# A graph network on one core: chunks, turned weights, copies and a residual put in another order and on other engines

## The chip, the cores and the metric

The kernel runs on one core of a Trainium2 chip. A core has TensorE (PE, products into PSUM), VectorE (DVE), ScalarE (ACT), GpSimd (POOL), and SyncE (SP), which here issues the transfers. Each engine takes its own instructions in the order in which they are written and waits on semaphores for the others. The metric is the device time of one execution in microseconds (us), lower is better.

## What is computed

The input x has 64 items of 128 rows and 512 nodes. Two graph layers follow each other, each with a residual and a layer norm over the nodes; the first one's graph is built from x itself (names as in the kernel):

```python
# layer 0; adj (128 x 128) is its weight, bias per row
x_norm = xn / max(norm(xn, axis=-1), 1e-12)              # xn: nodes, items, rows
S = einsum('nbl,mbl->nm', x_norm, x_norm) / B            # 512 x 512 likeness of nodes
A = S where it is among the k = 153 largest of its row (self left out), else 0
deg = A.sum(axis=0); An = rsqrt(deg)[:, None] * A * rsqrt(deg)[None, :]
out = einsum('sd,sbl->dbl', An, einsum('nbl,lo->nbo', xn, adj)) + bias
h = layernorm(x + out)
# layer 1, on h: two graphs of the 128 rows of each item
z_l = h @ W_lang.T; z_g = h @ W_grav.T; v = h @ W_V.T
K = w * rownorm(relu(cos(z_l, z_l))) + (1 - w) * rownorm(exp(-dist2(z_g) / (2 sigma^2)))  # causal
out = layernorm(h + (K @ v) @ W_O.T)
```

## The kernel before

Float32 operands are split in two float16 parts, high and low, and a product is three matmuls (`three`, lines 265 to 267): high by high, high by low, low by high. ScalarE mostly writes the high part, VectorE or GpSimd the low one (raw less high). The program has three stages; within a stage every engine's order is written out by hand.

1. **First pass** (to about 101 us). x comes in 16 chunks of 4 items (each chunk 4 slices of 128 x 512, `xn_h`, `xn_l`). PE's `rows_01` adds rows 0 and 1 of the block matrix S (banks 0, 1) chunk by chunk, as chunks are normalised.
2. **The stage of this change** (to about 204 us). PE finishes the diagonal blocks of rows 0 and 1 (`finish_diagonal`, lines 553 and 554: it adds the cross products high by low and their transpose, which ScalarE has copied out, `cross_out`, line 1007). ScalarE writes S (`s_out`, line 1002). PE turns five blocks (`turn`, line 559) and ScalarE copies them (line 1031). Then comes the **second pass**: `gram` for rows 2 and 3 of all 16 chunks, from what lies in SBUF (lines 523, 538, 544, 545, in the banks named pair23). Beside it VectorE searches the 153 largest entries of rows 0 and 1 (`pick(0)`: mean and deviation, whose root ScalarE takes, `deviation`, line 1026; three counts, line 1452; the eight next ones out, lines 1498 to 1507; a number loaded in a register, line 1526 is the first instruction behind it; then a loop) and makes A (`keep`, line 1550). Magnitudes of the inputs go over PE twice (lines 618 and 622) and give the scales (line 1568), after which ScalarE splits W_V and W_O (lines 1046, 1048), the adjacency, and group 0's x (lines 1058, 1063), with low parts by GpSimd (line 414). With the second pass done, rows 2 and 3 are finished in the same way and searched (`fill` lines 1585 to 1592, `pick(1)`, `keep(1)`). Beside that search PE turns W_grav (`turn_weight`, line 667; `less_high`, line 673, leaves the low part in the bank), makes W_V x W_O (`vo_product`, out by `vo_out`, lines 1133 and 1135), x times adjacency (`first_project`, out by lines 1074 and 1077), the upper blocks of W_grav's own product (`upper_product`), and sums the degrees (line 870). `needs_along` (line 610) turns the numbers that the search needs for its register. Behind the degrees (DVE line 1599) A is scaled and split, W_lang is turned, `mix_nodes` multiplies x's products with A, and group 0's y is made: bias and scale by ScalarE (`add_bias`, line 1098), x added by GpSimd (`residual`, line 438), statistics (line 1692), two factors, norm (line 1188), PE turns h (line 723), ScalarE and VectorE split it (lines 1278, 1880).
3. **16 groups of 4 items** (`body`) for the second layer and the next group's first layer. Here the first step that needs another engine's late work is group 1's x: high part by ScalarE (line 1083), low part by VectorE (line 1392), then `project_group`.

SP's transfers that lie in the stage: the first x (line 308) once W_V's low part is made, and the same x again into `xg[0]` (line 310) once the second pass is done.

## Time and profile before

| | us |
|---|---|
| median of 3 runs | 951.38 |
| lowest, highest | 951.23, 953.14 |
| profiled execution | 956.53 |
| its span | 954.8 |
| PE busy | 921.0 |
| VectorE busy | 752.5 |
| ScalarE busy | 535.4 |
| GpSimd busy | 312.8 |
| mean granted clock of PE | 0.989 |

The span goes from the first to the last instruction of the profiled execution. The matmul's own end is modelled in these records, and consecutive ones overlap: where PE is not waiting, the distance between starts is what a step costs. The granted clock is a share of 2.4 GHz; 0.5 is 1.2 GHz. The name in brackets behind a row of the timeline is the instruction whose end released the row's first one, with the idle time of the engine before it.

### The profile page before, as it was taken

The page shows a single profiled execution, that of the slowest core. Times are in us where ns is not written, and L with a number is a line of the kernel's source. Part 1 is how long each engine was busy: PE and PEld are TensorE (multiplying, and loading weights), DVE is VectorE, ACT ScalarE, POOL GpSimd, SP SyncE. Part 2 cuts the span into 40 slices and gives each one's busy share as a digit, 9 for nine tenths or more (in the row PEclk, how much of TensorE's full clock was granted, in tenths as well). Part 3 has the DMA queues.
Part 4 walks back from the last instruction along what each step waited for, and adds up shares of the span by engine and source line. Part 5 has one row for each costly group of instructions (what it writes and reads, how often), then busy time and mean ns, then how long its engine had stood idle before and what let it go on. Part 6 is the DMA issues. An engine that isn't in the chain of part 4 may idle for free.

```text
span 954.8 us, 19036 instructions
## 1 busy us (share of the span) xinstructions
PE 921.0 (96%) x6858; PEld 542.5 (57%) x6858; DVE 752.5 (79%) x1716; ACT 535.4 (56%) x976; POOL 312.8 (33%) x435
## 2 busy tenths in 40 slices
PE   8999899899999999999999999999999999999993
PEld 7777787455555555556464646455555455555451
DVE  5887488768888888878787888888887878786766
ACT  6887556685555555555546464646373636463531
POOL 5888162244040404040505050505050504040410
PEclk9999899999999999999999999999999999999997
DMA  7554120001323232314141413232222323231211
GB/s 301 187 204 150 43 90 25 34 32 21 80 67 78 67 83 60 95 48 109 34 120 28 115 33 109 40 103 46 96 53 90 57 86 60 85 56 45 56 45 44
DMA packets 101848, 75.84 MB, mean 79 GB/s; under 512 B 80560, under 2 KB 80688, under 8 KB 99888
## 3 DMA queue, kind: packets, MB, share of 16 engines
q1 hardware_dynamic: 101808, 75.32, 27.4%
q8 instruction: 24, 0.39, 0.2%
q14 instruction: 16, 0.13, 0.0%
HBM read 38.86 MB, written 16.78 MB: 58 GB/s over the span
## 4 chain that ended last, share of the span: by engine, by line
issue 51%; PE 21%; POOL 14%; DVE 8%; ACT 5%; DMA 1%; POOLq 1%; DVEq 0%; ACTq 0%
POOL arena L438 6%; PE bank L265 2%; PE bank L267 2%; PE bank L266 2%; PE bank L538 2%; POOL arena L443 2%; POOL arena L477 2%; PE bank L545 1%; PE bank L544 1%; ACT arena L1188 1%; POOL rn_parts L460 1%; DVE stats L1692 1%; POOL part_rest L458 1%; PE bank L508 1%; PE pair L265 1%
## 5 line engine op out<-in xcount | busy, mean ns | idle before, releaser
L265 PE MATMUL bank<-arena 128*128 128x512 f16 (+2 forms) x1056 | 293.8, 302 | 7.3 <-DVE arena L1746 2.7
L267 PE MATMUL bank<-arena 128*128 128x512 f16 (+2 forms) x1056 | 293.5, 302 | 0.0
L266 PE MATMUL bank<-arena 128*128 128x512 f16 (+2 forms) x1056 | 293.5, 302 | 0.0
L265 PE MATMUL pair<-arena 128*128 128x512 f16 (+1 forms) x400 | 151.1, 378 | 0.0
L266 PE MATMUL pair<-arena 128*128 128x512 f16 (+1 forms) x400 | 150.8, 377 | 0.0
L267 PE MATMUL pair<-arena 128*128 128x512 f16 (+1 forms) x400 | 150.7, 377 | 0.0
L265 PEld LDWEIGHTS bank<-arena 128*128 128x128 f16 x1056 | 103.5, 98 | 69.4 <-DVE arena L1746 5.0
L267 PEld LDWEIGHTS bank<-arena 128*128 128x128 f16 x1056 | 103.7, 98 | 63.3 <-issue 0.3
L266 PEld LDWEIGHTS bank<-arena 128*128 128x128 f16 x1056 | 103.7, 98 | 54.7 <-issue 0.3
L460 POOL TENSOR_TENSOR sq_parts<-cf,zero 128x4 bf16<-128x4 f32 x16 | 3.3, 208 | 399.4 <-DVE cf L1795 399.4
L438 POOL TENSOR_TENSOR arena<-arena 128x512 f32<-128x512 f32 x64 | 81.0, 1267 | 60.2 <-ACT arena L1098 59.8
L1199 ACT ACTIVATE arena<-bank 128x512 f16<-128x512 f32 x64 | 37.6, 589 | 96.7 <-PE bank L267 96.7
L443 POOL TENSOR_TENSOR arena<-arena 128x512 f16<-128x512 f32 x60 | 69.3, 1156 | 55.6 <-ACT arena L1193 53.6
L406 POOL TENSOR_TENSOR arena<-arena 128x512 f16<-128x512 f32 x64 | 72.8, 1160 | 21.4 <-ACT arena L976 21.4
L267 PEld LDWEIGHTS pair<-arena 128*128 128x128 f16 x400 | 39.1, 98 | 46.5 <-issue 0.3
L1746 DVE SCALAR_TENSOR_TENSOR arena<-bank,arena 128x512 f16<-128x512 f32 x64 | 43.9, 688 | 27.1 <-ACT arena L1199 27.1
L265 PEld LDWEIGHTS pair<-arena 128*128 128x128 f16 x400 | 39.1, 98 | 45.5 <-issue 0.5
L266 PEld LDWEIGHTS pair<-arena 128*128 128x128 f16 x400 | 39.2, 98 | 42.8 <-issue 0.5
L1188 ACT ACTIVATE arena<-arena,ln 128x512 f32<-128x512 f32 x64 | 51.3, 804 | 18.1 <-DVE ln L1718 18.1
L1392 DVE SCALAR_TENSOR_TENSOR arena<-arena,up 128x512 f16<-128x512 f32 x60 | 43.8, 774 | 19.3 <-ACT arena L1083 19.3
L1204 ACT ACTIVATE arena<-bank 128x512 f16<-128x512 f32 x32 | 19.1, 596 | 69.3 <-PE bank L267 69.3
L1692 DVE BATCH_NORM_STATS2 stats<-arena 128x6 f32<-128x512 f32 x64 | 44.1, 690 | 9.1 <-POOL arena L438 8.9
(344 smaller groups left out, 1943.0 us busy)
## 6 DMA issues: line engine op xcount, KB each, us to landing
arena<-in_x SPq DMA_DIRECT2D x32, 1024.0 KB, 5.5
out_dram<-arena SPq DMA_DIRECT2D x15, 1024.0 KB, 4.3
arena<-arena SPq DMA_TRANSPOSE x75, 3.2
arena<-in_x SPq DMA_DIRECT2D x2, 512.0 KB, 4.6
arena<-in_w_grav_t SPq DMA_DIRECT2D x1, 1024.0 KB, 7.3
arena<-in_w_lang_t SPq DMA_DIRECT2D x1, 1024.0 KB, 5.2
arena<-in_w_v SPq DMA_DIRECT2D x1, 1024.0 KB, 8.2
arena<-in_w_o_t SPq DMA_DIRECT2D x1, 1024.0 KB, 9.1
```

Source lines behind the costliest of these rows:

```text
L265: pe.matmul(dst, ah, bh, start=start, stop=False)
L266: pe.matmul(dst, ah, bl, start=False, stop=False)
L267: return pe.matmul(dst, al, bh, start=False, stop=stop)
L406: pool.tensor_tensor(xn_l[:, c * CL + t, :], xc[c % SLOTS][:, t, :], xn_h[:, c * CL + t, :], ALU.subtract).then_inc(s["xn_l_ready"], 1)
L438: pool.tensor_tensor(y[:, b, :], y[:, b, :], xg[slot][:, b, :], ALU.add).then_inc(s["y_ready"], 1)
L443: pool.tensor_tensor(h_l[:, b, :], h[slot][:, b, :], h_h[:, b, :], ALU.subtract).then_inc(s["hl_ready"], 1)
L1188: act.activation(h[slot][:, b, :], y[:, b, :], ACT.Identity, scale=ln1[:, 3, b:b + 1], bias=ln1[:, 4, b:b + 1]).then_inc(s["h_ready"], 1)
L1199: act.activation(z_h[i][:, E_ORDER[n], :, :], bank[n][:].rearrange("p (b n) -> p b n", b=GB), ACT.Copy, scale=U_DOWN).then_inc(done, 1)
L1204: act.activation(half_h[i], bank[4 + i][:].rearrange("p (b n) -> p b n", b=GB), ACT.Copy, scale=HALF_DOWN).then_inc(done, 1)
L1392: low = dve.scalar_tensor_tensor(x_l[:, b, :], xg[slot][:, b, :], up[:, 5:6], x_h[:, b, :], ALU.mult, ALU.subtract)
L1692: dve.bn_stats(stats[:, b, :], y[:, b, :]).then_inc(s["stat1_steps"], 1)
L1746: dve.scalar_tensor_tensor(z_l[i][:, e, :, :], bank[n][:].rearrange("p (b n) -> p b n", b=GB), U_DOWN, z_h[i][:, e, :, :], ALU.mult, ALU.s ...
```

## The change

- PE: rows 2 and 3 of chunk 0 are computed before the diagonals of rows 0 and 1, those of chunk 1 between diagonals and turns. The magnitude steps follow chunks 4 and 6 (were 2 and 4), the needs' transpose chunk 12 (was 9). W_grav's first turned weight stands before the diagonals of rows 2 and 3, the second before their turn. W_V's products 0 to 2 come ahead of x's products, which all stand behind the transpose of the second search's needs and use banks 0 to 3.
- ScalarE: four of the six fills of the second search's work area; x's scaling and high part behind S and a turned weight's high part; W_V's products out ahead of x's; the second search's root behind both; the bias added to group 0's x in place, in two steps of two items; in the last part, the turned h's first two high parts ahead of the norms of items 2 and 3, and W_lang's first copy behind them.
- VectorE: in a search, the register's steps are put between the two replacements, and the load beside the second; two of six fills stay; group 0's y is one step each from the bank (product times scale plus biased x), and the columns of constants are moved between these steps.
- GpSimd: no residual for group 0.
- SP: nothing in its code.

On PE, from the end of the first pass (rows 0, 1: bank0, bank1) into the second pass (pair23). L553 and L554 are the diagonals, L559 the turns. Before:

```order
L553 MATMUL bank0<-rinv_rep,ident 128x128
L554 MATMUL bank0<-ident,rinv_rep 128x128
L553 MATMUL bank1<-rinv_rep,ident 128x128
L554 MATMUL bank1<-ident,rinv_rep 128x128
L559 MATMUL bank7<-ident,arena 128x128
L559 MATMUL bank5<-ident,arena 128x128 x2
L559 MATMUL bank6<-ident,arena 128x128 x2
L538 MATMUL pair23<-arena 128x256
L523 MATMUL pair23<-arena 128x128
L544 MATMUL pair23<-arena 128x128
```

After, where L550 and L551 are the diagonals and L556 the turns; the rows left out repeat the slices of a chunk:

```order
L535 MATMUL pair23<-arena 128x256
L520 MATMUL pair23<-arena 128x128
L541 MATMUL pair23<-arena 128x128
...
L550 MATMUL bank0<-rinv_rep,ident 128x128
L551 MATMUL bank0<-ident,rinv_rep 128x128
L550 MATMUL bank1<-rinv_rep,ident 128x128
L551 MATMUL bank1<-ident,rinv_rep 128x128
L520 MATMUL pair23<-arena 128x128
L535 MATMUL pair23<-arena 128x256
...
L556 MATMUL bank7<-ident,arena 128x128
L556 MATMUL bank5<-ident,arena 128x128 x2
L556 MATMUL bank6<-ident,arena 128x128 x2
```

Two chunks of the second pass moved ahead, one before the diagonals and one before the turns.

On ScalarE, from x's scaling to the root of the second search (L1026, the last row). Before:

```order
L1058 ACTIVATE arena<-arena,up 128x2048
L1007 ACTIVATE rinv_rep<-pair23 128x128 x2
L1063 ACTIVATE arena<-arena 128x2048
L1002 ACTIVATE arena<-pair23 128x256
L1002 ACTIVATE arena<-pair23 128x128
L1070 ACTIVATE arena<-bank7 128x128
L1111 ACTIVATE arena<-bank4 128x512
L1111 ACTIVATE arena<-bank5 128x512
L1026 ACTIVATE guess<-guess 128x2
```

After, from the cross copies to the same root, now L1023; L1139 and L1142 are x, L1103 the low parts of two turned weights, L1121 and L1123 W_V's first product:

```order
L999 ACTIVATE arena<-pair23 128x128
L1027 ACTIVATE arena<-pair23 128x128
L1027 ACTIVATE arena<-bank7 128x128
L1136 ACTIVATE arena<-bank7 128x128
L1099 ACTIVATE arena<-bank5 128x512
L1139 ACTIVATE arena<-arena,up 128x2048
L1142 ACTIVATE arena<-arena 128x2048
L1103 ACTIVATE arena<-bank4 128x512
L1103 ACTIVATE arena<-bank5 128x512
L1121 ACTIVATE arena<-bank0 128x512
L1123 ACTIVATE arena,vo_magn<-arena 128x512
L1023 ACTIVATE guess<-guess 128x2
```

x's two passes, once ahead of S, are behind it, and they, the low parts and W_V's product now stand ahead of the root.

On VectorE, group 0's y behind the split of A. Before, where y comes from GpSimd (L1692 is its statistics):

```order
L1647 TENSOR_TENSOR arena<-arena 128x1280
L1651 TENSOR_REDUCE vo_top<-bank7 4x1
L1653 TENSOR_SCALAR vo_top<-vo_top 4x1
L1655 TENSOR_SCALAR vo_diag<-ident,vo_top 4x4
L1656 TENSOR_SCALAR col<-pw 128x1
...
L1668 TENSOR_SCALAR col<-col 128x1
L1692 BN_STATS stats<-arena 128x6 x2
L1699 BN_AGGR mv<-stats 128x2 x2
L1703 TENSOR_SCALAR ln1<-mv 128x2
```

After (L1870 is y, L1677 its statistics):

```order
L1653 TENSOR_TENSOR arena<-arena 128x1280
L1870 SCALAR_TENSOR_TENSOR arena<-bank0,col,arena 128x512
L1870 SCALAR_TENSOR_TENSOR arena<-bank1,col,arena 128x512
L1879 TENSOR_REDUCE vo_top<-bank7 4x1
L1881 TENSOR_SCALAR vo_top<-vo_top 4x1
L1883 TENSOR_SCALAR vo_diag<-ident,vo_top 4x4
L1677 BN_STATS stats<-arena 128x6 x2
L1684 BN_AGGR mv<-stats 128x2 x2
L1688 TENSOR_SCALAR ln1<-mv 128x2
L1870 SCALAR_TENSOR_TENSOR arena<-pair23,col,arena 128x512
```

Y's steps are new in the row and stand ahead of their statistics; the constants have moved back.

The diff, cut to what is spoken of:

```diff
--- before.py
+++ after.py
...
-        first_bank = [bank[1], bank[2], bank[3], bank[6]]
+        first_bank = bank[0:GB]
...
-            for b in range(GB):
-                residual(0, 0, b)
...
+
+            gram(0, range(2, KB), first=True)
             finish_diagonal(0)
             finish_diagonal(1)
+            gram(1, range(2, KB))
             pe.wait_ge(s["S_ready"], 2)
             turn(bank[7][:, 0:P], 0, 1).then_inc(s["S_turned"], 1)
...
-            for c in range(NC):
-                gram(c, range(2, KB), first=(c == 0), last=(c == NC - 1))
-                if c == 2:
+            for c in range(2, NC):
+                gram(c, range(2, KB), last=(c == NC - 1))
+                if c == 4:
...
-                if c == 4:
+                if c == 6:
...
-                if c == 9:
+                if c == 12:
                     pe.wait_ge(s["S_ready"], 5)
                     needs_along(0)
...
-            finish_diagonal(2)
-            finish_diagonal(3)
-            pe.wait_ge(s["S_ready"], 6)
-            turn(bank[7][:, P:2 * P], 2, 3).then_inc(s["S_turned"], 1)
...
-            def first_project(b):
-                pe.wait_ge(s["adj_l_ready"], 1)
-                pe.wait_ge(s["x_l_ready"], 1)
-                pe.wait_ge(s["S_ready"], 7)
-                project_x(0, b, first_x_h, first_x_l, first_bank[b])
...
-            def vo_product(d):
-                pe.wait_ge(s["w_l_ready"], 2)
-                wait(pe, s["xw_h_ready"], d)
...
+            turn_weight(1, 0)
+            finish_diagonal(2)
+            finish_diagonal(3)
+            turn_weight(1, 1)
+            pe.wait_ge(s["S_ready"], 6)
+            turn(bank[7][:, P:2 * P], 2, 3).then_inc(s["S_turned"], 1)
...
+            def first_project(b):
+                pe.wait_ge(s["adj_parts"], 3)
+                pe.wait_ge(s["x_l_ready"], 1)
+                pe.wait_ge(s["vo_out"], b + 1)
+                project_x(0, b, first_x_h, first_x_l, first_bank[b])
...
+            def vo_product(d):
+                pe.wait_ge(s["w_l_ready"], 2)
+                if d == 2:
+                    pe.wait_ge(s["S_ready"], 8)
...
                 if i:
-                    pe.wait_ge(s["vo_out"], d + 1)
+                    pe.wait_ge(s["xw_h_ready"], d + 1)
                 elif d == KB - 1:
                     pe.wait_ge(s["vo_steps"], 4)
...
-            turn_weight(1, 0)
-            turn_weight(1, 1)
             vo_product(0)
             less_high(1, 0)
             less_high(1, 1)
-            first_project(0)
-            first_project(1)
+            vo_product(1)
             turn_weight(1, 2)
             turn_weight(1, 3)
-            pe.wait_ge(s["S_ready"], 8)
+            vo_product(2)
             degrees(range(0, 2))
-            first_project(2)
-            first_project(3)
-            vo_product(1)
             less_high(1, 2)
             less_high(1, 3)
-            vo_product(2)
-            pe.wait_ge(s["xw_h_ready"], KB)
+            vo_product(3)
             needs_along(1)
-            vo_product(3)
+            for b in range(GB):
+                first_project(b)
             for d in range(KB):
                 upper_product(1, d)
             degrees(range(2, KB))
...
+            def fill_out(dst, src, scale=1.0):
+                act.activation(dst, src, ACT.Copy, scale=scale).then_inc(s["work_23_ready"], 1)
+
             act.wait_ge(s["S_turned"], 3)
             for dst, src in ((S[:, 1, 0:P], bank[7][:, 0:P]), (S[:, 2, 0:2 * P], bank[5][:, 0:2 * P]),
                              (S[:, 3, 0:2 * P], bank[6][:, 0:2 * P])):
                 act.activation(dst, src, ACT.Copy).then_inc(s["S_ready"], 1)
+            fill_out(work[:, 2, 0:2 * P], bank[5][:, 0:2 * P])
+            fill_out(work[:, 3, 0:2 * P], bank[6][:, 0:2 * P])
...
-            act.wait_ge(s["w_in2"], 32)
-            act.activation(first_x, first_x, ACT.Copy, scale=up[:, 5:6]).then_inc(s["w_scaled"], 1)
-            cross_out(2)
-            cross_out(3)
-            act.wait_ge(s["w_scaled"], 3)
-            act.wait_ge(s["w_l_ready"], 2)
-            act.activation(first_x_h, first_x, ACT.Copy).then_inc(s["x_h_ready"], GB)
-
-            act.wait_ge(s["gram_full"], 3)
-            s_out(S[:, 2, 2 * P:], bank[2][:, 0:2 * P])
-            act.wait_ge(s["gram_full"], 4)
-            s_out(S[:, 3, 3 * P:], bank[3][:, 0:P])
-            act.wait_ge(s["S_turned"], 4)
-            act.activation(S[:, 3, 2 * P:3 * P], bank[7][:, P:2 * P], ACT.Copy).then_inc(s["S_ready"], 1)
...
+            cross_out(2)
+            cross_out(3)
             turned_high(1, 0)
+            act.wait_ge(s["gram_full"], 3)
+            s_out(S[:, 2, 2 * P:], bank[2][:, 0:2 * P])
+            act.wait_ge(s["gram_full"], 4)
+            s_out(S[:, 3, 3 * P:], bank[3][:, 0:P])
+            fill_out(work[:, 2, 3 * P:NODES], bank[2][:, P:2 * P], S_SCALE)
+            act.wait_ge(s["S_turned"], 4)
+            fill_out(work[:, 3, 2 * P:3 * P], bank[7][:, P:2 * P])
+            act.activation(S[:, 3, 2 * P:3 * P], bank[7][:, P:2 * P], ACT.Copy).then_inc(s["S_ready"], 1)
             turned_high(1, 1)
-            deviation(1)
+            act.wait_ge(s["w_in2"], 32)
+            act.activation(first_x, first_x, ACT.Copy, scale=up[:, 5:6]).then_inc(s["w_scaled"], 1)
+            act.wait_ge(s["w_scaled"], 3)
+            act.wait_ge(s["w_l_ready"], 2)
+            act.activation(first_x_h, first_x, ACT.Copy).then_inc(s["x_h_ready"], GB)
             turned_low(1, 0)
             turned_low(1, 1)
-            first_xw_high(0)
-            first_xw_high(1)
+            vo_out(0)
+            deviation(1)
             turned_high(1, 2)
             turned_high(1, 3)
-            first_xw_high(2)
-            first_xw_high(3)
-            vo_out(0)
+            vo_out(1)
+            vo_out(2)
             turned_low(1, 2)
             turned_low(1, 3)
-            vo_out(1)
-            vo_out(2)
             vo_out(3)
+            for b in range(GB):
+                first_xw_high(b)
+
+
+            def x_biased(items):
+                act.activation(xg[0][:, items, :], xg[0][:, items, :], ACT.Identity,
+                               bias=bias_c[:]).then_inc(s["x_biased"], 1)
+
+            act.wait_ge(s["x_in0"], 16)
+            act.wait_ge(s["small_in"], 64)
+            x_biased(slice(0, HALF))
             for d in range(KB):
                 upper_out(1, d)
+            x_biased(slice(HALF, GB))
             act.wait_ge(s["deg_in"], 1)
             act.activation(deg_t[:], deg_m[:], ACT.Sqrt).then_inc(s["deg_root"], 1)
...
-            act.wait_ge(s["d_ready"], 1)
-            add_bias(0, 0)
-            add_bias(0, 1)
             turned_low(0, 2)
             turned_low(0, 3)
-            add_bias(0, 2)
             first_roots(0, 0)
             first_norm(0, 0, 0)
             first_norm(0, 0, 1)
-            add_bias(0, 3)
+            first_roots(0, 1)
+            hT_high(0)
+            hT_high(1)
+            first_norm(0, 0, 2)
+            first_norm(0, 0, 3)
+            hT_high(2)
+            hT_high(3)
             act.wait_ge(s["vo_steps"], 5)
             act.activation(vo_scale[:, 1:2], vo_scale[:, 0:1], ACT.Ln).then_inc(s["vo_root"], 1)
             act.wait_ge(s["vo_root"], 1)
             act.activation(vo_scale[:, 0:1], vo_scale[:, 1:2], ACT.Exp, scale=0.5).then_inc(s["vo_root"], 1)
-            first_roots(0, 1)
-            upper_out(0, 0)
-            first_norm(0, 0, 2)
-            first_norm(0, 0, 3)
-            for b in range(GB):
-                hT_high(b)
-            for d in range(1, KB):
+            for d in range(KB):
...
-                    dve.wait_ge(ps, n)
-                    for t in range(2):
-                        dve.match_replace(w[t], top8[:, t, :], w[t], TAKEN).then_inc(ps, 1)
-                    n += 2
...
+                needs = bank[6][0:1, 0:2 * P]
+                found, loaded = (extra_i[0:1, 2 * pair + i:2 * pair + i + 1] for i in range(2))
                 dve.wait_ge(s["most_ready"], pair + 1)
...
+                dve.tensor_scalar(found, extra_f[0:1, pair:pair + 1], 7.0 - 8 * ROUNDS, 8.0, ALU.add,
...
+                dve.match_replace(w[0], top8[:, 0, :], w[0], TAKEN).then_inc(ps, 1)
+                dve.wait_ge(ps, n + 1)
+                dve.tensor_scalar(loaded, found, 0xF8, None, ALU.bitwise_and).then_inc(ps, 1)
+                dve.match_replace(w[1], top8[:, 1, :], w[1], TAKEN).then_inc(ps, 1)
+                n += 4
+                dve.wait_ge(ps, n - 1)
+                extra = dve.value_load(loaded, min_val=8, max_val=K_NEAR)
                 dve.wait_ge(ps, n)
...
             filled = s["work_23_ready"]
-            dve.wait_ge(s["S_ready"], 5)
             for r in range(2, KB):
-                dve.tensor_copy(work[:, r, 0:2 * P], S[:, r, 0:2 * P]).then_inc(filled, 1)
-            dve.wait_ge(s["S_ready"], 6)
-            dve.tensor_tensor(work[:, 2, 2 * P:3 * P], S[:, 2, 2 * P:3 * P], self_mark[:], ALU.add).then_inc(filled, 1)
-            dve.tensor_copy(work[:, 2, 3 * P:NODES], S[:, 2, 3 * P:]).then_inc(filled, 1)
-            dve.wait_ge(s["S_ready"], 7)
-            dve.tensor_tensor(work[:, 3, 3 * P:NODES], S[:, 3, 3 * P:], self_mark[:], ALU.add).then_inc(filled, 1)
+                mine = slice(r * P, (r + 1) * P)
+                dve.wait_ge(s["S_ready"], 4 + r)
+                dve.tensor_tensor(work[:, r, mine], S[:, r, mine], self_mark[:], ALU.add).then_inc(filled, 1)
...
-            dve.tensor_copy(work[:, 3, 2 * P:3 * P], S[:, 3, 2 * P:3 * P]).then_inc(filled, 1)
...
+            def first_y(b):
+                dve.wait_ge(s["mix_ps"], b + 1)
+                dve.scalar_tensor_tensor(y[:, b, :], bank[b][:], c1(ALPHA_C), xg[0][:, b, :], ALU.mult,
+                                         ALU.add).then_inc(s["y_ready"], 1)
+
+            dve.wait_ge(s["d_ready"], 1)
+            dve.wait_ge(s["x_biased"], 2)
+            first_y(0)
+            first_y(1)
+            vs = s["vo_steps"]
+            dve.wait_ge(s["vo_turned"], 1)
...
             first_stats(0, 0)
             first_stats(0, 1)
             first_moments(0, 0)
+            first_y(2)
...
             first_factors(0, 0)
...
+            first_stats(0, 2)
...
+            first_y(3)
+            first_stats(0, 3)
+            first_moments(0, 1)
...
-            first_stats(0, 3)
-            first_moments(0, 1)
             first_factors(0, 1)
...
```

## Rows read from the trace of the kernel before

**Rows 1.** The page, engines and granted clock in 40 slices

```profile
PE 921.0 (96%) x6858; PEld 542.5 (57%) x6858; DVE 752.5 (79%) x1716; ACT 535.4 (56%) x976; POOL 312.8 (33%) x435
...
PEclk9999899999999999999999999999999999999997
```

**Rows 2.** PE's waits, 96 to 215 us: total, times, longest

```profile
PE bank L559 <- ACT arena L1002: 2.2, 2, 1.1
...
PE bank L553 <- ACT rinv_rep L1007: 1.6, 1, 1.6
PE bank L667 <- ACT arena L1115: 1.3, 1, 1.3
...
PE pair L553 <- ACT rinv_rep L1007: 1.0, 1, 1.0
```

**Rows 3.** Two stretches: busy time of engines, PE's clock, DMA

```profile
104.00:111.00 7.00, 5.85 (x45) 5.30 (x44) 4.19 (x17) 4.30 (x10) 0.00 (x0) 0.52 0.00 1
...
193.00:196.50 3.50, 3.50 (x26) 2.83 (x24) 2.71 (x8) 2.12 (x7) 0.00 (x0) 0.51 0.00 0
```

**Rows 4.** Timeline of PE, 101 to 114 us: start, length, instruction

```profile
102.96 0.49 PE L553 MATMUL bank<-rinv_rep,ident 128*128 128x128 f32 x2 [1.58 <-ACT rinv_rep L1007]
...
105.27 1.33 PE L559 MATMUL bank<-ident,arena 128*128 128x128 f32 x5 [1.15 <-ACT arena L1002]
106.39 0.42 PE L538 MATMUL pair<-arena 128*128 128x256 f16 x1
...
110.98 0.33 PE L538 MATMUL pair<-arena 128*128 128x256 f16 x1
...
113.47 0.27 PE L538 MATMUL pair<-arena 128*128 128x256 f16 x1
...
113.86 0.27 PE L538 MATMUL pair<-arena 128*128 128x256 f16 x1
```

**Rows 5.** Timeline of VectorE, 117 to 166 us

```profile
117.04 0.17 DVE L1568 TENSOR_SCALAR pw<-bank 128x8 int32<-128x8 int32 x1 [1.24 <-PE bank L622]
...
130.37 0.07 DVE L1526 MEMSET cut<- 128x16 f32 x1 [1.00 <-DVE extra_i L1519]
...
136.44 0.49 DVE L1585 COPY arena<-arena 128x256 f32<-128x256 f32 x2
...
140.19 1.28 DVE L1421 BATCH_NORM_STATS2 row_stats<-arena 128x6 f32<-128x512 f32 x2
...
143.48 0.16 DVE L1445 SCALAR_TENSOR_TENSOR guess<-guess 128x2 f32<-128x2 f32 x1 [0.27 <-ACT guess L1026]
...
147.06 0.54 DVE L1458 SCALAR_TENSOR_TENSOR guess<-guess 128x2 f32<-128x2 f32 x1
...
162.22 1.29 DVE L1550 SCALAR_TENSOR_TENSOR arena<-arena 128x512 f32<-128x512 f32 x2
165.86 0.16 DVE L1599 TENSOR_SCALAR deg_m<-bank 128x4 f32<-128x4 f32 x1 [2.35 <-PE bank L870]
```

**Rows 6.** Timeline of ScalarE, 102 to 144 us

```profile
102.65 0.42 ACT L1007 ACTIVATE rinv_rep<-bank 128x128 f32<-128x128 f32 x2
...
133.21 2.00 ACT L1058 ACTIVATE arena<-arena,up 128x2048 f32<-128x2048 f32 x1 [7.05 <-DMA arena<-in_x]
...
143.25 0.20 ACT L1026 ACTIVATE guess<-guess 128x2 f32<-128x2 f32 x1 [2.82 <-DVE guess L1443]
```

**Rows 7.** Timeline of all engines, 185 to 205 us

```profile
186.94 1.27 POOL L438 TENSOR_TENSOR arena<-arena 128x512 f32<-128x512 f32 x1 [3.73 <-ACT arena L1098]
...
188.24 0.69 DVE L1692 BATCH_NORM_STATS2 stats<-arena 128x6 f32<-128x512 f32 x1 [2.88 <-POOL arena L438]
...
191.65 1.36 PE L723 MATMUL pair<-ident,arena 128*128 128x128 f32 x8 [2.18 <-ACT arena L1188]
...
198.16 2.54 ACT L1083 ACTIVATE arena<-arena,up 128x512 f16<-128x512 f32 x4
...
204.17 0.22 PE L265 MATMUL bank<-adj_h,arena 128*128 128x128 f16 x1 [1.05 <-DVE arena L1746]
```

80 lines of the change are left out of this document (36 added, 44 removed).

## The prediction

> **What bounds the kernel now.** I read the page first: TensorE (PE) is busy for 96% of the span [rows 1], so an edit is worth time only where PE stands still or runs at its lower clock. The page's row of clocks is full but for a few slices. So I listed PE's waits over 96 to 215 us, the stretch that the diff touches: 2.2 us in two waits for S, 1.6 and 1.0 for the cross products, 1.3 for a weight's low part [rows 2], and two more that the timeline shows, 2.18 for the third h and 1.05 for group 1's x [rows 7]. The table of stretches gives the price of the clock [rows 3]: 0.52 granted from 104 to 111 us (mostly 1.2 GHz, after PE had idled 1.58 us and while it idled 1.15), 0.51 from 193 to 196.5 us (after 2.18 us idle). Other slices here show 2.4 GHz. The stretch divides where the search of nodes ends and VectorE takes the degrees, at 165.86 [rows 5]: parts 1 to 3 lie ahead of it, part 4 behind.
>
> **Part 1, chunks ahead of diagonals and turns.** Before, PE ends the first pass at about 101.4 (102.96 less 1.58), waits for ScalarE's cross copies (begun at 102.65 [rows 6]), adds diagonals from 102.96, waits for S, turns from 105.27, and starts the second pass at 106.39 [rows 4]. Its items (a 128-row slice of a chunk) stand 0.39 us apart at full clock (113.47 to 113.86); at half, six take 4.59 us, from 106.39 to 110.98 [rows 4]. Now chunk 0 (4 items, 1.56 us) fills 101.4 to 102.95; diagonals end near 104.1; chunk 1 (1.56 us) covers ScalarE's two copies of S, done at 105.2; five turns at full clock take 0.55 us. PE is then at 106.1 with 8 items done, where it had 6 done at 110.98. That is 4.9 + 2 x 0.39 = **5.7 us**: the two idle spells and half the time at half clock. No work is removed. The second pass ends at 128.7 instead of 134.4.
>
> TensorE's two magnitude steps move from the ends of chunks 2 and 4 to those of 4 and 6, at 110.8 and 114.0. VectorE waited 1.24 us for the second, until 117.04 [rows 5]; now it has it at 114.5. Scales, ScalarE's weights, GpSimd's low parts and the first x's load come **2.5 us** earlier.
>
> **Part 2, turned weights round the diagonals of rows 2 and 3.** PE waited 1.0 and 1.1 us there [rows 2]. Now one turned weight (0.9 us) stands before the diagonals, one before the last turn, and ScalarE has nothing ahead of the cross copies, since x's two passes (2.0 and 1.9 us, from 133.21 [rows 6]) are behind S. Both waits go: **2.1 us**, and S is whole at 132.3 instead of 138.3. W_V's products then stand next (0.216 us a step, 12 steps each); their low parts are ready near 130.3, PE asks at 131.6.
>
> **Part 3, the search's copies and the register.** VectorE's fills run from 136.44 to 140.19 [rows 5]; four of six go to ScalarE at some 0.3 us each, two adds of 0.3 us stay. The register load left VectorE 1.00 us idle in the first search [rows 5] (0.7 in the second); beside a replacement of 0.68 us most of it goes. The first search ends at 136.5 - 2.5 - 0.9 = 133.1, the second begins at 133.7 instead of 140.19, and asks for its root 3.0 us on, at 136.7.
>
> **The new wait.** On ScalarE the root stands behind the rest of S (to 132.3), a high part 0.6, x scaled 2.0, x's high part 1.9, two low parts 1.06, and W_V's first product out 1.25. That makes 139.1, and VectorE idles 2.4 us. From the root the search took 143.48 to 163.51, 20.0 us [rows 5]. Less 0.7 for the register: 158.5. GpSimd's low parts stretch VectorE's small steps beside them (L1458 takes 0.54 at 147.06 [rows 5], 0.16 without); more or fewer of them may now fall on the search, -0.3 to +1.3 us. I take +0.5, nearer the row's own stretch of small steps: A is ready at 159.0, the last row's degrees (0.9) end at 159.9 against 165.8, 5.9 us, and with the small wait behind it I take **5.8 us**. By PE's work alone it would be 5.7 + 2.1 = 7.8; the rest turns into waits: PE reaches the transpose of the second search's needs at 146.6, with W_V's four products done, and the needs come near 148 (8.9 us behind the root). Behind that transpose x's products are queued, then W_grav's. A second wait, some 0.5 us, stands before the last degrees.
>
> ScalarE's queue can be weighed by itself. The trace shows it idle 2.8 us before the root at 143.25 [rows 6], with all behind it held. The Trainium skill (TensorE: Matmul & The Clock Gate, section "Architectural detail: the array is 16× 32×32, not 1× 128×128") says that ScalarE's and VectorE's queues are strictly first in, first out, which speaks against the root's new place. The trace agrees. Were it otherwise, the root would come 2.4 us sooner, PE's work would bound, and the sum below would be 2 us larger.
>
> **Part 4, group 0's y by VectorE.** Here I keep the clock of before. PE's products run to 189.3 as now (1.3 us idle for the weight's low part stays [rows 2]). y(3) went mix, ScalarE, GpSimd (1.27 us from 186.94), statistics at 188.24, factors, norms; PE had the third h at 191.65 after 2.18 us [rows 7]. Now VectorE makes y(3) in one step of 0.7 us once the mix (184.1) and its own queue are through: 184.3 to 185.0, statistics 0.7, moments 0.55, root 0.5 on ScalarE, factors 0.8: 187.6. ScalarE copies two turned h first (to 188.1), then norms the third: 188.9. PE wants it at 189.3. So the wait goes, and with it, I hold, the drop of the clock: turns 0.9 and W_lang's last two products (12 x 0.109 + 12 x 0.055 = 1.96) end at 192.2 instead of 196.48, **4.3 us**. The bias goes into x ahead of time, two ScalarE steps; no row has this form, so I bound each by 0.8 (one item's y with bias) and 2.0 us (x scaled, four items [rows 6]) and take 1.1, two items being nearer the middle. They lie before the degrees, where ScalarE has over 2 us free.
>
> Given back: W_lang's copies (0.64 + 0.57 + 0.44 + 0.28), its high part (1.3) and x's high parts are a chain on ScalarE, now behind the last turned h (191.05) and a root pair (0.4). x's high parts start at 194.5 instead of 198.16 [rows 7], **3.6 us** earlier. VectorE's low parts (4.44 us) follow, and only then is PE let into group 1's x products (204.17 before [rows 7]). PE's wait there grows from 1.05 to 1.8 us; 3.6 of the 4.3 us remain. From there the engines stand to each other as before.
>
> **Sum.** 5.8 + 3.6 = 9.4 us. The profiled execution took 956.53 us (span 954.8) and would take 947.1; the median of the three runs is 951.38, 0.5% less, so **942.0 us**.
>
> **Rivals.** (a) The clock drops anew: at PE's new idle of 1.5 us near 147, or at the 1.3 us in the mix. For: 1.58 and 1.15 us did it at 104. Against: 1.0 and 1.1 us near 136 and 1.3 us near 169 did not [rows 1, 2]. Price: 7 us at 0.52 is 3.4 us [rows 3], less up to 1 us of slack before the degrees: 944.4 to 945.4.
> (b) The third h is late all the same: should the third norm slip 1 us behind the turned h's copies, PE idles and the clock may fall. Then 1 to 2 of the 3.6 us stay: 944. Against: 0.4 us of slack, and y's steps no longer cross three engines.
> (c) More than forecast: GpSimd disturbs less, the waits near 147 and 159 shrink. The bound is PE's work, 7.8 + 4.3 = 12.1 us: 939.3.
> (d) Slower: the root hangs on the first x's load, now ahead of it on ScalarE. The load lands at 130.7 (133.2 before, where it ended a wait of 7 us [rows 6]), and is needed at 132.9. The load of xg[0] is issued at 128.8, into its flight. Each us of landing after 132.9 costs one; from 142.3 the gain is gone, and at 144.5 the kernel takes 953.6. A whole second flight of some 5 us costs 3 only, so this is unlikely.
> (e) The edits do not bite: part 1's lead ends as idle before A and part 4's before x's products; under 1.9 us, 950.
>
> **Chances.** Forecast (940.5 to 943.5) 0.55, (a) 0.15, (b) 0.12, (c) 0.11, (d) 0.02, (e) 0.05. The range 938.8 to 946.5 holds the first four with their tails. A measurement here can tell 0.2% (1.9 us) from no change: faster 0.94 (all but (d) and most of (e)), same 0.04, slower 0.02.
>
> **What would show it.** Clock 1.00 from 104 to 111; second pass ends near 128.7; scales near 114.5; root near 139 with VectorE idle 2 to 3 us before it; PE idle 1 to 2 us before the needs' transpose; degrees taken near 160; no idle before the third turned h and clock 1.00 behind it; group 1's x products near 194.8. I am wrong if the clock falls in either place, if A comes after 161, or if the later groups shift against one another.

## The result and the profile after

The changed kernel took 947.13 us (median of five executions, 945.65 to 947.4) beside 951.38 us for the kernel before (five executions, 951.08 to 953.81). The medians are 4.3 us apart; the ratio over all executions is 0.9943, 95% interval 0.9926 to 0.9959, which is 5.4 us. It is faster. The prediction said 942.0 us with a range of 938.8 to 946.5, a gain of 9.4 us. So the sign was right and the size about twice too large. The median of 947.13 lies 0.6 us above the range; the ratio, applied to the 951.38 us from which the forecast was made, gives 946.0 us, inside it.

Five executions are few here. Over all 84 executions of before in this document the median is 953.3 us (three of the five above stood at 951.1 to 951.4), and over the eleven of the changed kernel it is 947.13: 6.2 us apart.

Yet the trace of after shows almost every step where the prediction put it. Its profiled execution took 945.65 us (span 943.9). The page, the answer to [rows 1]:

```profile
span 943.9 us, 18952 instructions
...
PE 915.0 (97%) x6858; PEld 538.8 (57%) x6858; DVE 750.7 (80%) x1716; ACT 535.5 (57%) x978; POOL 307.6 (33%) x431
...
PEclk9999999999999999999999999999999999999997
```

The one dip left is the last slice. PE's waits from 96 to 215 us, the answer to [rows 2] (total, times, longest):

```profile
PE bank L645 <- ACT arena L1103: 1.3, 1, 1.3
PE bank L265 <- DVE arena L1731: 1.3, 1, 1.3
PE bank L873 <- DVE arena L1561: 1.0, 1, 1.0
PE bank L610 <- DVE guess L1489: 0.8, 1, 0.8
PE bank L265 <- DVE arena L1640: 0.4, 1, 0.4
```

The waits for S, for the cross copies and for the third h are gone. The new ones are those for the needs' transpose (L610) and for the last degrees (L873). The wait for the weight's low part (L645) stays, and the one before group 1's x (L1731) has grown from 1.05 to 1.25. The timelines of after (start, length, instruction, idle time before it and what ended it), from PE, VectorE, ScalarE, and then the later stretch:

```profile
102.53 0.49 PE L550 MATMUL bank<-rinv_rep,ident 128*128 128x128 f32 x2
...
105.07 0.71 PE L556 MATMUL bank<-ident,arena 128*128 128x128 f32 x5
...
128.12 1.11 PE L645 MATMUL bank<-arena 128*128 128x128 f32 x8
```

```profile
114.02 0.17 DVE L1579 TENSOR_SCALAR pw<-bank 128x8 int32<-128x8 int32 x1 [0.40 <-PE bank L622]
...
133.53 1.29 DVE L1428 BATCH_NORM_STATS2 row_stats<-arena 128x6 f32<-128x512 f32 x2
...
138.31 0.31 DVE L1452 SCALAR_TENSOR_TENSOR guess<-guess 128x2 f32<-128x2 f32 x1 [2.14 <-ACT guess L1023]
...
159.37 0.16 DVE L1605 TENSOR_SCALAR deg_m<-bank 128x4 f32<-128x4 f32 x1 [1.44 <-PE bank L873]
```

```profile
138.09 0.19 ACT L1023 ACTIVATE guess<-guess 128x2 f32<-128x2 f32 x1
...
187.56 2.54 ACT L1071 ACTIVATE arena<-arena,up 128x512 f16<-128x512 f32 x4
```

```profile
177.61 0.75 DVE L1870 SCALAR_TENSOR_TENSOR arena<-pair,col,arena 128x512 f32<-128x512 f32 x1 [0.68 <-PE pair L267]
...
193.56 0.22 PE L265 MATMUL bank<-adj_h,arena 128*128 128x128 f16 x1 [1.25 <-DVE arena L1731]
```

Against the profiled execution of before, degrees are taken 6.5 us earlier (165.86, now 159.37) and group 1's x starts 10.6 us earlier (204.17, now 193.56), which is the difference of the two spans, 10.9 us, but for 0.3. So the two traces differ by what the prediction summed, and a little more, while the medians differ by 4.3 us (6.2 over all executions). The experiments had to say which of the two is the change.

Three groups of runs were made, each with its own executions of before beside it. Executions of before differ by up to 6 us (950.87 to 956.87), and the granted clock that each records goes roughly with the time; I give the range and the clocks with each. Three executions (1071.02 us in p1_only, 1928.19 and 3358.0 us of before) lie far outside and are left out of every median, ratio and range.

### The profile page after: what moved, and what is told of

It reads as the page before. It is cut to its first block, busy times and chain, and to the rows that moved or that the text cites. A ratio compares the mean times of both kernels' runs of the same rounds, so it can differ in the third digit from the quotient of the medians.

```text
span 943.9 us, 18952 instructions
## 1 busy us (share of the span) xinstructions
PE 915.0 (97%) x6858; PEld 538.8 (57%) x6858; DVE 750.7 (80%) x1716; ACT 535.5 (57%) x978; POOL 307.6 (33%) x431
## 4 chain that ended last, share of the span: by engine, by line
PE 62%; DVE 14%; ACT 4%; issue 3%; DMA 1%; POOL 1%; DVEq 0%; SPq 0%; ACTq 0%; POOLq 0%
PE bank L265 13%; PE bank L267 12%; PE bank L266 12%; PE pair L265 7%; PE pair L267 7%; PE pair L266 7%; DVE arena L1731 4%; DVE arena L1724 2%; DVE arena L1399 1%; PE bank L778 1%; ACT arena L1071 1%; DMA arena<-arena 1%; ACT arena L1210 1%; PE bank L753 1%; PE bank L752 1%
## 5 line engine op out<-in xcount | busy, mean ns | idle before, releaser
L438 POOL TENSOR_TENSOR arena<-arena 128x512 f32<-128x512 f32 x60 | 76.0, 1267 | 29.5 <-ACT arena L1086 29.2
L1731 DVE SCALAR_TENSOR_TENSOR arena<-bank,arena 128x512 f16<-128x512 f32 x64 | 43.9, 687 | 27.7 <-ACT arena L1210 27.7
L414 POOL TENSOR_TENSOR arena<-arena 128x256 f16<-128x256 f32 x45 | 30.8, 722 | 73.1 <-ACT arena L1117 33.5
```

The source lines that it names most:

```text
L414: last = pool.tensor_tensor(dst[:, mine, :], raw[:, mine, :], hi[:, mine, :], ALU.subtract)
L438: pool.tensor_tensor(y[:, b, :], y[:, b, :], xg[slot][:, b, :], ALU.add).then_inc(s["y_ready"], 1)
L1731: dve.scalar_tensor_tensor(z_l[i][:, e, :, :], bank[n][:].rearrange("p (b n) -> p b n", b=GB), U_DOWN, z_h[i][:, e, :, :], ALU.mult, ALU.s ...
```

## The same two kernels again

**The kernel before, unchanged.** No edit.

> The kernel before, unchanged, to see how its clock varies from execution to execution. Clock theory (the profiled execution of before, 956.53 us, was 5.2 us over its median because TensorE's clock fell twice, at 104 and at 193 us, and most executions lack one or both drops): the mean granted clock varies between about 0.989 and 0.995 over executions, and the time with it, near 951.4 at the higher clocks and 953 to 957 at 0.989. Profiling theory (the 5 us are a cost of recording, the drops occur in every execution): the clock is 0.989 in all and the profiled execution is again 5 us over the median.

Twelve executions took 950.87 to 955.74 us, median 952.65; ratio to the runs of before beside it 0.9992 (0.9979 to 1.0006). The three at a granted clock of 0.994 took 951.4 and the one at 0.990 took 955.74; the lowest, 950.87, had 0.993, so the mean clock orders the times only roughly. Of the 79 executions of before whose clock is on record, 19 stand at 0.994 (951.2 to 952.2 us, median 951.4). Of the other 60, all but the one of 950.87 took 952.19 us or more. The clock theory was borne out: the profiled one took 951.37 us (span 949.6) at 0.994, so recording does not cost the 5 us. Its stretches (length, busy time of PE, weight load, VectorE, ScalarE, GpSimd, then PE's clock, DMA share, GB/s), the answer to [rows 3], and its waits:

```profile
104.00:111.00 7.00, 6.15 (x91) 5.97 (x92) 5.18 (x19) 4.12 (x10) 0.00 (x0) 1.00 0.00 1
193.00:196.50 3.50, 3.50 (x18) 1.58 (x17) 2.73 (x3) 3.50 (x6) 3.38 (x4) 1.00 0.00 0
```

```profile
PE bank L559 <- ACT arena L1002: 2.2, 2, 1.2
PE pair L723 <- ACT arena L1188: 2.2, 1, 2.2
PE bank L553 <- ACT rinv_rep L1007: 1.6, 1, 1.6
...
PE pair L553 <- ACT rinv_rep L1007: 0.7, 1, 0.7
```

Its rows of PE and VectorE, to be held against [rows 4], [rows 5] and [rows 7]:

```profile
102.54 0.49 PE L553 MATMUL bank<-rinv_rep,ident 128*128 128x128 f32 x2 [1.57 <-ACT rinv_rep L1007]
104.85 0.77 PE L559 MATMUL bank<-ident,arena 128*128 128x128 f32 x5 [1.15 <-ACT arena L1002]
...
198.96 0.22 PE L265 MATMUL bank<-adj_h,arena 128*128 128x128 f16 x1 [0.48 <-DVE arena L1746]
```

```profile
162.30 0.16 DVE L1599 TENSOR_SCALAR deg_m<-bank 128x4 f32<-128x4 f32 x1 [2.34 <-PE bank L870]
```

The idle spells are nearly the same as in [rows 2], but the clock stays at its upper level (2.4 GHz) behind them, where [rows 3] has 0.52 and 0.51. VectorE has the scales at 113.84 instead of 117.04, degrees at 162.30 instead of 165.86, and group 1's x starts at 198.96 instead of 204.17. Of these 5.2 us, 0.4 stand already at the first diagonals (102.54 instead of 102.96), ahead of either drop; 3.1 go to the first drop and 1.6 to the second, 4.8 us together. 956.53 less 951.37 is 5.16. So the gap between the profiled execution and the median, which I had turned into a factor of 0.995, was those two drops and a start 0.4 us later.

**The changed kernel, unchanged.** No edit.

> The changed kernel, unchanged. Clock theory: 945.6 where the clock is 0.994, up to 947.5 at 0.991, the difference being a drop somewhere outside 0 to 200 us or at a new idle spell; ratio to before near 0.994 to 0.996, since before's median has at most one drop. Profiling theory: all profiles at 0.994, the times spread without regard to the clock.

Six executions took 945.43 to 949.79 us, median 946.8; ratio 0.9928 (0.9912 to 0.9944). Three of them at 0.994 took 945.4 to 946.3; the profiled one, at 0.989, took 949.79. Its waits are those of after (0.8 before the needs, 1.1 before the last degrees), and its stretches show what they cost this time:

```profile
158.00:160.00 2.00, 2.00 (x15) 2.00 (x15) 0.46 (x1) 0.20 (x1) 0.00 (x0) 0.76 0.44 32
160.00:162.00 2.00, 2.00 (x11) 2.00 (x11) 1.12 (x8) 0.21 (x1) 0.00 (x0) 0.50 0.72 269
162.00:164.00 2.00, 2.00 (x11) 2.00 (x11) 0.37 (x1) 0.60 (x1) 0.00 (x0) 0.50 0.59 227
```

This is rival (a), the clock that drops anew, in some executions and not in others, though behind the degrees' idle of 1.1 us and not behind the needs'. Group 1's x starts at 196.57 instead of 193.56. Of these 3.0 us, 0.5 stand already at the scales (114.54 instead of 114.02), so the drop took 2.5 (the rival's price was 3.4 less up to 1 of slack). The whole execution is 4.1 us longer; about 1.1 of it lies behind the last groups, where the clock was 0.55 from 930 to 935 us (0.72 in after). The ratio was expected at 0.994 to 0.996, with one drop at most in before's median; it came out lower, and the 947.5 us expected as the highest was passed.

Compared at the same mean clock of 0.994, before takes 951.2 to 952.2 us (19 executions, median 951.4) and the changed kernel 945.4 to 946.3 (five, median 945.65). So the change is worth 5.7 us at that clock, where neither profiled execution has a drop in this stage, and 6.2 in the medians of all executions.

## Parts of the change, one at a time

**Part 1 alone**, on the kernel before:

```diff
+            gram(0, range(2, KB), first=True)
             finish_diagonal(0)
             finish_diagonal(1)
+            gram(1, range(2, KB))
...
-            for c in range(NC):
-                gram(c, range(2, KB), first=(c == 0), last=(c == NC - 1))
-                if c == 2:
+            for c in range(2, NC):
+                gram(c, range(2, KB), last=(c == NC - 1))
+                if c == 4:
```

> The kernel before with part 1 alone (chunks 0 and 1 of the second pass ahead of diagonals and turns, magnitude steps and needs' transpose later by as many chunks). In the trace without a drop the two idle spells are 1.57 and 1.15 us. If PE's lead reaches the end: fastest execution 951.35 - 2.7 = 948.6. If the search's chain on VectorE takes part of it back: the second search begins when ScalarE is through with x (133.2 + 2.0 + 1.9, less what comes earlier), so 949 to 950. Rival (the lead ends as idle before A): 951.3. Median under that of before by 1 to 3 us, since the drop at 104 can't occur.

Eleven executions took 952.81 to 957.27 us, median 954.23; ratio 1.0011 (0.9997 to 1.0026): no gain. PE's waits and the stretches behind them:

```profile
PE pair L553 <- ACT rinv_rep L1009: 4.8, 1, 4.8
```

```profile
130.00:135.00 5.00, 1.73 (x8) 1.73 (x8) 3.89 (x11) 3.94 (x4) 0.36 (x1) 0.60 0.55 200
135.00:140.00 5.00, 4.84 (x26) 3.79 (x26) 4.37 (x11) 2.14 (x6) 4.74 (x8) 0.71 0.00 0
```

The whole lead became one idle of 4.8 us: ScalarE has its copies for the diagonals of rows 2 and 3 behind the first x's scaling, which waits for its load until 131.06 (129.66 in before_again, so 1.4 of the 4.8 us are the load's). The clock fell during that idle, and degrees came at 164.69, later than without the edit. The expectation of 948.6 to 950 was missed; the rival, that the lead ends as an idle, was right.

**The change without part 1** (the same edit undone in the changed kernel):

> The changed kernel without part 1: idle spells of 1.6 and 1.15 us near 102 to 105 return, with the clock free to fall there. Fastest execution 945.4 + 0.9 to 2.7 = 946.3 to 948.1 (less than 2.7 if TensorE's idle of 0.82 and 1.04 us before needs and degrees shrinks in exchange); median 2 to 5 us over that of the changed kernel, with executions at clock 0.991 or less in more than half.

Twelve executions took 948.56 to 953.67 us, median 951.24; ratio 0.9979 (0.9964 to 0.9994). At a clock of 0.994 it took 948.6 to 948.8, over the 946.3 to 948.1 expected. In its profiled execution (948.56) degrees are taken at 162.25, against 159.37 with part 1. The rows of VectorE say why parts 2 and 3 alone bring nothing to that point:

```profile
134.51 1.29 DVE L1426 BATCH_NORM_STATS2 row_stats<-arena 128x6 f32<-128x512 f32 x2 [0.88 <-ACT arena L1134]
...
141.19 0.31 DVE L1450 SCALAR_TENSOR_TENSOR guess<-guess 128x2 f32<-128x2 f32 x1 [4.04 <-ACT guess L1021]
```

VectorE begins its second search 2.1 us sooner than in before (136.64), and then waits 4.04 us for the root, because S is late and ScalarE has x's two passes between S and the root. Part 1 is worth 2.9 us at the degrees, 2.9 in the time at a clock of 0.994 (948.6 less 945.65) and 4.4 in the medians (951.24 less 946.8), in the changed kernel only.

**Parts 1 and 2, on the kernel before** (the changed kernel without ScalarE's fills, the register's load ahead, and y by VectorE). Lines of the edit that take part 3 away, against the changed kernel:

```diff
-            fill_out(work[:, 2, 0:2 * P], bank[5][:, 0:2 * P])
-            fill_out(work[:, 3, 0:2 * P], bank[6][:, 0:2 * P])
...
             for r in range(2, KB):
...
+                dve.tensor_copy(work[:, r, 0:2 * P], S[:, r, 0:2 * P]).then_inc(filled, 1)
```

> The kernel before with parts 1 and 2 alone (no fills by ScalarE, no register load ahead, y by ScalarE and GpSimd as before). Part 1 alone gained nothing (TensorE's lead ended as one idle of 4.82 behind ScalarE's scaling of the first x, which waited for its load). Theory: part 2 is what lets the lead through, because ScalarE takes the rows of S ahead of the first x's scaling; then the idle of 4.8 at 133 is gone, degrees are taken at 160.4 to 161.5 where the kernel before has 162.3, and an undisturbed execution takes 949.2 to 950.3, against 951.4 of the kernel before. Rival: the wait goes on to the first x itself (its high and low parts, needed by the first products of x), so degrees stay at 162 to 163 and the time at 951 to 951.8.

Ten executions took 951.09 to 956.39 us, median 954.14; ratio 0.9993 (0.9974 to 1.0012). The idle of 4.8 us is gone, as the theory said, but two others stand in its place:

```profile
PE pair L729 <- ACT arena L1190: 2.2, 1, 2.2
PE bank L613 <- DVE guess L1484: 2.0, 1, 2.0
PE bank L876 <- DVE arena L1553: 2.0, 1, 2.0
```

```profile
160.00:165.00 5.00, 5.00 (x26) 5.00 (x27) 1.49 (x8) 0.80 (x2) 0.00 (x0) 0.54 0.69 210
...
190.00:195.00 5.00, 4.95 (x33) 3.67 (x32) 2.90 (x8) 3.57 (x11) 0.00 (x0) 0.66 0.13 52
```

PE now waits for VectorE's search, before the needs and before the degrees. Behind the second of these the clock was 0.54 from 160 to 165 us, and behind the third h's wait 0.66. Degrees at 161.87 are only 0.4 us ahead of before; 0.6 more went to the half clock (PE's step for the last degrees took 2.56 us, 1.95 in after). The total gained nothing: the range forecast for an undisturbed execution (949.2 to 950.3) was not reached by any of ten; the lowest took 951.09, at 0.991.

**The change without part 3** (the edit whose lines stand at parts 1 and 2, with part 4 kept):

> The changed kernel without part 3: the six fills of the second search stand on VectorE again and the register's value is loaded behind the last two replacements. The changed kernel takes 945.4 at a granted clock of 0.994. Theory, each part keeps its own share: the loads cost VectorE's chain some 0.6 us in each search (they idled 1.00 and 0.72 before, 0.38 and nothing in the changed kernel) and the fills that follow the last rows of S some 0.6 more, so BN_STATS of the second search begins 1 to 1.5 later than 133.5, degrees are taken at 160.4 to 161 where it was 159.37, group 1's x begins at 194.5 to 195, and an undisturbed execution takes 946.3 to 947. Rival, part 3 is covered: the work it takes off VectorE ends before the wait for ScalarE's root at 138, so that the root's wait (2.14) shrinks by what the fills cost and degrees come at 159.4 to 159.8: 945.4 to 945.8.

Eight executions took 948.37 to 950.4 us, median 948.78; ratio 0.9946 (0.9928 to 0.9964). None had a clock above 0.991; at 0.991 four took 948.4 to 948.8 where the changed kernel took 947.3 to 947.4, so part 3 is worth about 1.3 us there, and 2.0 in the medians (948.78 less 946.8). The profiled execution started 1.5 us late (scales at 115.55, behind a clock of 0.91 in the first 20 us). Less that, the root comes 1.1 us and the degrees 1.4 us later than in the changed kernel: what I expected (160.4 to 161), and not the rival's nothing. VectorE's timeline has a reason that I had not counted:

```profile
138.23 0.53 DVE L1437 TENSOR_SCALAR guess<-guess 128x2 f32<-128x2 f32 x1
138.79 0.58 DVE L1440 TENSOR_TENSOR guess<-guess 128x2 f32<-128x2 f32 x1
139.41 0.59 DVE L1443 SCALAR_TENSOR_TENSOR guess<-guess 128x2 f32<-128x2 f32 x1
140.03 0.60 DVE L1446 TENSOR_SCALAR guess<-guess 128x2 f32<-128x2 f32 x1
...
162.34 0.16 DVE L1603 TENSOR_SCALAR deg_m<-bank 128x4 f32<-128x4 f32 x1 [1.44 <-PE bank L873]
```

The four steps before the root take 0.53 to 0.60 us each here, beside GpSimd's low parts, and 0.16 to 0.17 in the changed kernel (135.41 to 136.17), where they are over as it starts (136.05). So without part 3 VectorE asks for its root 2.9 us later (1.1 for its later start, the rest for these steps), and the wait of 2.14 us, which part 3 had left it, takes up all but 1.1 of that.

**The change without part 4** (group 0's y by ScalarE and GpSimd as before):

```diff
+            for b in range(GB):
+                residual(0, 0, b)
...
+            act.wait_ge(s["d_ready"], 1)
+            add_bias(0, 0)
+            add_bias(0, 1)
...
-            first_y(0)
-            first_y(1)
```

> The changed kernel without part 4: group 0's y by ScalarE and GpSimd again, x without bias, ScalarE's order before the turned h's copies as before. If part 4's gain is the idle spell of 2.2 us less what is given back (clock not falling in most executions): 1.5 to 2.5 us slower than the changed kernel, 948.0 to 949.5. If the clock falls behind that idle spell in every execution: 3.6 us or more, 950.5 to 951.5. The profile shows TensorE idle some 2.2 us before the third turned h in either case.

Twelve executions took 947.96 to 953.26 us, median 950.67; ratio 0.9968 (0.9954 to 0.9982). At 0.994 it took 948.6 and 948.7; the lowest had 0.991. The idle before the third turned h is back at 2.2 us. In the profiled execution (951.27, at 0.991) the clock fell twice, to 0.52 from 160 to 162 us, and behind the idle before the third h to 0.60 from 187 to 189 and 0.55 from 189 to 191. Part 4 is worth 3.0 us at 0.994 (948.6 less 945.65), over the 1.5 to 2.5 expected for a clock that holds, and 3.9 in the medians. The drop behind this idle is not in every execution, against the rival.

Put side by side, with the scales taken at 113.8 to 114.2 in all of these (start in us; before is its undisturbed execution). The kernel without part 3, whose scales came at 115.55, is given less 1.53 us:

| kernel | root back on VectorE | degrees taken | what stands before them |
|---|---|---|---|
| before | 139.92 | 162.30 | S late, fills behind it |
| part 1 alone | 141.32 | 164.69 | ScalarE waits for x's load, clock falls |
| parts 2 and 3, with 4 | 141.19 | 162.25 | root behind x's passes |
| parts 1 and 2 | 139.27 | 161.87 | VectorE's fills and slow small steps, clock falls |
| parts 1 and 2, with 4 | 139.38 | 160.81 | the same, clock full until the degrees |
| all | 138.31 | 159.37 | root 2.14 late, needs 0.8, degrees 1.0 |

Part 1 alone, and parts 2 and 3 without it, gain nothing at the degrees. Parts 1 and 2 gain 0.4 us in one kernel and 1.5 in the other (the difference is mostly the half clock, 0.6 us, and one small step of VectorE behind the root, 0.72 us against 0.15). All three gain 2.9, with part 4 or without it (159.45 in no_p4). Part 2, 3 or 4 alone, and 1 with 3, were not tried.

## The root, and the idle spells

**The root ahead of W_V's first product out**, in the changed kernel:

```diff
+            deviation(1)
             vo_out(0)
-            deviation(1)
```

> The changed kernel with the second search's root one step earlier on ScalarE, ahead of W_V's first product out (1.25 us). My theory (the search waits for its root behind ScalarE's queue, and TensorE behind the search): VectorE's idle before the root shrinks from 2.1 to 0.9 us, TensorE's idle of 0.8 before the needs' transpose goes and that of 1.0 before the last degrees shrinks, 0.7 to 1.2 us faster in the profile, about 946.0 as median. Rival (the root's wait is covered): no change, TensorE waits elsewhere, 947.1.

Five executions took 944.84 to 947.22 us, median 945.77; ratio 0.9925 (0.9907 to 0.9942). In the profiled one (944.84) VectorE's wait for the root is 0.89 instead of 2.14 us:

```profile
137.10 0.30 DVE L1452 SCALAR_TENSOR_TENSOR guess<-guess 128x2 f32<-128x2 f32 x1 [0.89 <-ACT guess L1023]
...
158.14 0.16 DVE L1605 TENSOR_SCALAR deg_m<-bank 128x4 f32<-128x4 f32 x1 [1.44 <-PE bank L873]
```

ScalarE began the root 1.23 us earlier (136.86 against 138.09), which is the one product out that had stood ahead of it (0.60, 0.63 and 0.19 us, overlapping). Degrees come 1.2 us and group 1's x 1.2 us earlier (192.35), the profiled time is 0.8 us lower (944.84 against 945.65), and PE's idle before the needs is gone while that before the degrees is 0.8 instead of 1.0. So ScalarE's order is what sets the root, as expected. The gain itself is read from the traces: the ratio's interval overlaps that of the changed kernel (0.9912 to 0.9944). The rule that the prediction cites from the Trainium skill (TensorE: Matmul & The Clock Gate, section "Architectural detail: the array is 16× 32×32, not 1× 128×128"), that ScalarE's queue is strictly first in, first out, agrees with this run.

**Filler products in before's idle spells.** 80 products of 128 columns, 26 before the first diagonals, 18 before the turns, 36 before the third h:

```diff
+            stay(26, bank[2])
             finish_diagonal(0)
...
+            stay(18, bank[2])
             pe.wait_ge(s["S_ready"], 2)
```

> The kernel before with 80 small products of a constant (128 columns of bfloat16 each, into a bank that is free, then overwritten) put where TensorE stands still: 26 before the first diagonals, 18 before the turns, 36 before the third turned h. They fill waits and lie on no path. Clock theory (before's executions of 952 to 956.4 us are those in which TensorE's clock fell behind these idle spells; those of 951.35 had none): nearly all executions at 951.4 with clock 0.994, none over 953. Rival (the drops come by themselves, or from the waits elsewhere): the spread of 951.35 to 956.4 stays.

Twelve executions took 953.06 to 955.77 us, median 954.18; ratio 1.0008 (0.9995 to 1.002): nothing gained, and the expectation (nearly all at 951.4) missed. The profiled execution, 955.27 us, kept its clock where the fillers stand and lost it elsewhere:

```profile
104.00:111.00 7.00, 6.85 (x104) 6.50 (x101) 5.21 (x19) 4.09 (x10) 0.00 (x0) 1.00 0.01 4
130.00:135.00 5.00, 2.75 (x27) 2.25 (x24) 3.51 (x11) 3.96 (x4) 0.00 (x0) 0.88 0.50 147
135.00:140.00 5.00, 4.50 (x19) 3.93 (x20) 4.39 (x11) 2.06 (x6) 4.75 (x8) 0.50 0.17 66
```

There PE had idled 2.1 us for the cross copies of rows 2 and 3, where before_again shows 0.7, since ScalarE could begin with the first x only at 131.04 (129.66 there): its load landed later, though it was issued at the same time (124.60 and 124.64). That wait, which I had counted as 1.0 us of plain idle, is another place where the clock can fall, and part 2 takes it away. Neither profile of before shows a drop there, so how often it costs before something is not shown. Nor is it shown why no execution with fillers took less than 953.06 us, where 8 of the 29 of before beside them took 951.3 to 952.2: one profile tells only where this execution lost its time, and the fillers themselves delayed nothing ahead of 130 us (scales at 113.81).

**Fillers in the waits that the changed kernel has left**, with the root ahead (12, 20 and 18 products before the degrees, before the third turned weight and before group 1's x):

```diff
+            pe.wait_ge(s["u_out"], 2)
+            stay(12, bank[0])
             degrees(range(2, KB))
```

> The changed kernel with the root ahead of W_V's first product out, and 50 such small products in the three waits that are left (12 before the last degrees, 20 before W_lang's third turned weight, 18 before group 1's x products). Clock theory: executions gather at 944.8 to 945.0, clock 0.994, median 0.8 to 1.9 us under that of the changed kernel, no execution over 946.5. Rival (small products do not hold the clock, or delay what follows): median 945.8 or more, spread as without them.

Six executions took 944.51 to 946.38 us, median 945.9; ratio 0.9919 (0.9901 to 0.9938). None is over 946.5, where the changed kernel and the one with the root ahead reached 949.8 and 947.2, but the median is no lower than with the root ahead alone (945.77). The expected gathering at 944.8 to 945.0 did not come. With six and five executions the difference to the root ahead alone can't be told from none. What varies in these six is not located; the profiled one (944.65) has its full clock up to 925 us and 0.58 from 925 to 930, where root_ahead has 0.85.

## Why the prediction was off, and where it was right

- **Part 1, 5.7 us.** The order came out as told: chunk 0 fills the wait (diagonals at 102.53, the same moment as before), turns at 105.07, second pass ended at 128.1 (128.7 forecast), clock 1.00. But of the 5.7 us, 2.8 were half-clock time that the undisturbed execution of before does not have. In that one, turns stand at 104.85 with no item done, now at 105.07 with eight (3.1 us): 2.9 us.
- **Scales 2.5 us earlier.** They came 3.0 us earlier than in the profiled execution of before, but all of it was clock and the later start. Against the undisturbed before (113.84) they are 0.2 us later (114.02).
- **Part 2, 2.1 us.** Both waits went (1.74 us in the undisturbed before). Its greater worth is that it lets part 1's lead through (p1_only against p12: idle of 4.8 us gone), though without part 3 VectorE's search gives most of it back.
- **Part 3.** Fills and load were put right in place; S was whole at 131.6, and the second search began at 133.53 (133.7 forecast). Worth 1.3 us in the time and 1.4 at the degrees, not separately forecast.
- **The new wait.** Root begun at 138.1, 139.1 forecast; VectorE idle 2.14 us, 2.4 forecast; the needs' wait 0.8 us, 1.5 forecast; degrees at 159.37, 159.9 forecast. This was the best-founded step, and root_ahead bears out the mechanism.
- **Part 4, 4.3 and 3.6 us.** No idle before the third turned h; last y at 177.61 and x's high parts at 187.56, where the forecast (194.5 in the clock of before, less 5.8) has 188.7. Without drops it is worth 3.0 us. The rest of the 4.3 us holds the second drop, which some executions have and others not.
- **The bias's two steps** took 1.13 and 1.14 us, 1.1 taken. **The wait before group 1's x** is 1.25 us, 1.8 forecast.
- **The sum.** Here is the step that was wrong. The profiled execution was to take 947.1 us, and an undisturbed one takes 945.65: as a forecast of where the instructions come to stand it was 1.5 us too high. But the sum was made from an execution that had lost 4.8 us to two drops and 0.4 to a later start, the drops were counted as gain, and then the median was reached by scaling with 0.995. The gap of 5.15 us between that execution and the median of 951.38 was mostly a list of two rows, [rows 3], not a percentage; it had to be taken off the gain. Done so, 9.4 less 5.2 is 4.2 us, or 947.2 us, where the measurement beside it says 4.3 and 947.13. That this comes so near is luck: the undisturbed gain is 5.7 us, and the one in the medians of all executions 6.2. For the second cause of the miss lies in the median itself. Three executions of before put it at 951.38, where 84 put it at 953.3, and 60 of 79 ran below the highest mean clock: most executions of before do lose time to drops, and the change takes some of them away. The time of 942.0 was too low for either reading.
- **Rival (a)** was named with the right price and treated as one case for all executions. It is a share of the executions, and it came behind another idle than the two that were named: after_again's profile has it behind the degrees' 1.1 us, after's has not. (b), (c), (d) and (e) did not come. The load of the first x landed in time, since x's scaling began at 131.97, right behind S and one high part. (e) is what happens to part 1 on its own.

## What to carry to other kernels

When the profiled execution is longer than the median, first look in its trace for what it has that the others lack; here the granted clock of two stretches accounted for 4.8 of the 5.16 us. Take the median over enough executions: three put it 1.9 us below that of all 84. Price an edit against an execution without it, and give the drops that it removes as a share of executions. A lead on one engine is worth what the next engine's queue lets through. So try each piece of a reordering alone, and also leave it out of the whole: part 1 gained nothing alone and cost 2.9 us when it was left out, because its lead has to pass ScalarE's queue and then VectorE's search.
